# A banded attention's mask: on VectorE with the maximum, or as accumulating matmuls in three of four head groups

## The reference

```python
# x: (4, 2048, 256); 16 heads of 16; WINDOW = 128, one global token
attend = abs(i - j) <= 128 | (i < 1) | (j < 1)
x = x + 0.5 * ffn(layernorm(x))      # top 2 of 8 experts; one with over 1280 tokens is dropped
h = layernorm(x)
q, k, v = (h @ W.T, split in heads, for W in (Wq, Wk, Wv))
logits = where(attend, q @ k.T / 4, -inf)
x = x + (softmax(logits) @ v, heads joined) @ Wo.T
x = x + 0.5 * ffn(layernorm(x))
```

## Time and profile before

| | |
|---|---|
| median of three runs | 870.89 us (870.79 to 871.8) |
| span of the profiled execution, first to last instruction | 867.2 us |
| mean granted TensorE clock | 0.997 |
| TensorE, VectorE, ScalarE, GpSimd busy | 94%, 87%, 73%, 56% |
| first strip's matmuls | at 26.4 us |
| last strip's matmuls | at 794.5 us |

### The profile page before, as it was taken

The page is one execution under the profiler, slowest core; times in us unless marked ns, Lnnn a source line. Parts: engine busy times, 40 slices in busy tenths (PEclk is TensorE's granted clock), DMA queues, the critical chain, the costliest instruction groups (busy, mean ns, idle before and its releaser), DMA issues. The chain is left out here.

```text
span 867.2 us, 50607 instructions
## 1 busy us (share of the span) xinstructions
PE 814.6 (94%) x21504; PEld 606.9 (70%) x21505; DVE 758.3 (87%) x2819; ACT 637.2 (73%) x1417; POOL 488.1 (56%) x874
## 2 busy tenths in 40 slices
PE   9798999999999999999999999898999999999894
PEld 8555667767777777667778777666778777766572
DVE  7898899989887899998987899998988889998785
ACT  2268888897877667998877666898777766888850
POOL 3212556675555557765554465675554556656763
PEclk9999999999999999999999999999999999999998
DMA  7722224432212344441213335352222335220113
GB/s 231 116 81 75 67 73 121 135 88 70 77 62 96 111 146 119 120 127 62 89 51 101 106 105 161 108 131 71 74 73 68 106 93 149 94 77 18 49 51 102
DMA packets 93191, 83.51 MB, mean 96 GB/s; under 512 B 17568, under 2 KB 92192, under 8 KB 92960
## 3 DMA queue, kind: packets, MB, share of 16 engines
q1 hardware_dynamic: 91360, 78.91, 30.1%
q10 hardware_dynamic: 1600, 1.31, 1.0%
HBM read 20.66 MB, written 8.39 MB: 33 GB/s over the span
## 5 line engine op out<-in xcount | busy, mean ns | idle before, releaser
L1105 ACT ACTIVATE probs<-bank 128x384 f32<-128x384 f32 (+1 forms) x1024 | 462.8, 480 | 146.8 <-PE bank L962 137.4
L1431 DVE CUSTOM_DVE_ANT_0 bank<-bank,con 128x288 f32<-128x288 f32 x1024 | 494.4, 518 | 53.2 <-PE bank L934 44.8
L934 PE MATMUL bank<-k_stack,q_stack 96*32 96x288 bf16 x4096 | 325.4, 288 | 10.7 <-DVE row_max L1431 5.7
L962 PE MATMUL bank<-q_stack,k_stack 99*32 99x288 bf16 (+2 forms) x4096 | 319.8, 285 | 16.0 <-ACT probs L1105 9.7
L980 PE MATMUL bank<-probs,v_sb 128*32 128x128 f32 x5888 | 305.4, 272 | 3.6 <-issue 1.5
L1218 POOL TENSOR_SCALAR_AFFINE_SELECT probs<-probs 128x512 f32<-128x512 f32 x240 | 154.8, 645 | 180.1 <-ACT probs L1105 179.5
L980 PEld LDWEIGHTS bank<-probs,v_sb 128*32 128x32 f32 x5888 | 192.1, 110 | 36.7 <-issue 5.3
L962 PEld LDWEIGHTS bank<-q_stack,k_stack 99*32 99x32 bf16 x4096 | 123.6, 95 | 79.7 <-ACT probs L1105 53.5
L934 PEld LDWEIGHTS bank<-k_stack,q_stack 96*32 96x32 bf16 x4096 | 127.3, 95 | 74.0 <-DVE row_max L1431 21.3
L1223 POOL TENSOR_SCALAR_AFFINE_SELECT probs<-probs 128x512 f32<-128x512 f32 x240 | 154.1, 642 | 19.3 <-ACT probs L1105 19.2
L823 PE MATMUL bank<-xnT,wqk_sb 128*32 128x256 f32 x2048 | 158.1, 379 | 0.6 <-DVE neg_max L1453 0.5
(11 more groups left out here) (126 smaller groups left out, 737.2 us busy)
## 6 DMA issues: line engine op xcount, KB each, us to landing
q_stack<-pieces SPq DMA_DIRECT2D x384, 64.0 KB, 2.7
k_stack<-pieces SPq DMA_DIRECT2D x364, 64.0 KB, 2.7
x_ring<-in_x SPq DMA_DIRECT2D x28, 512.0 KB, 4.5
out_x<-x_ring SPq DMA_DIRECT2D x16, 512.0 KB, 3.9
attn<-in_x SPq DMA_DIRECT2D x4, 512.0 KB, 6.0
wback_sb<-in_wback SPq DMA_DIRECT2D x8, 256.0 KB, 6.0
k_stack<-pieces ACTq DMA_DIRECT2D x20, 64.0 KB, 3.6
q_stack<-neg_max SPq DMA_DIRECT2D x48, 16.0 KB, 2.3
```

Of the source, the lines that this page charges most:

```text
L934: last = pe.matmul(a_ring[i % len(a_ring)][SP * s:SP * (s + 1), 0:WIN], q_stack[g % 2][0:KROWS, h, q:q + SP], k_stack[g % 2][0:KROWS, h, q ...
L962: last = pe.matmul(b_ring[i % len(b_ring)][SP * s:SP * (s + 1), start:final], k_stack[g % 2][0:SROWS, h, WINDOW + P * j + SP * s:WINDOW + ...
L1105: act.activation(probs[:, j % 4, h, c0:c1], b_ring[i % len(b_ring)][:, c0:c1], ACT.Exp, scale=LOGIT_SCALE).then_inc(S["exp_ready"], 1)
L1431: dve.tensor_tensor_reduce(out=a_ring[i % len(a_ring)][:, 0:WIN], in0=a_ring[i % len(a_ring)][:, 0:WIN], in1=mask, scale=1.0, scalar=con[: ...
```

## The change

In the first, third and fourth head group of each batch (`g % NG != 1`), `A` no longer closes the bank after the four score matmuls. Further matmuls accumulate the mask on them: the stationary operand is a bf16 identity (a quarter of its columns for each quarter of the partitions), the moving one the bf16 mask. They cover only the columns in which the mask isn't zero. For a middle tile these are the first and the last 32 of 288 columns, in one matmul of 2 x 32. For a group's first tile they are 128 columns and 32, in two matmuls, and for its last tile 32 and 128. VectorE then does a plain maximum (`tensor_reduce`) and writes nothing back. The second group (`g % NG == 1`) keeps the old instruction.

ScalarE makes the two bf16 copies (identity and masks) at the start. The band's DMA has a semaphore of its own for that, at its old place in the queue. TensorE's first `A` waits for the two copies; VectorE's first `A` no longer waits for the set-up loads. The order of events is unchanged.

```diff
+        ident_half = sb("ident_half", [P, P], BF16)
+        band_half = sb("band_half", [P, 3, WIN], BF16)
...
+        def masked_by_products(g):
+            return g % NG != 1
+        def mask_of(t):
+            return 0 if t == 0 else 2 if t == NT - 1 else 1
+        def both_edges(strip):
+            return strip.rearrange("p (b c) -> p b c", c=SP)[:, 0:2 * WINDOW // SP + 1:2 * WINDOW // SP, :]
+        def mask_parts(t):
+            if t == 0:
+                return lower_half, upper_edge
+            if t == NT - 1:
+                return lower_edge, upper_half
+            return both_edges,
...
-                                (con[:, C_BAND:C_PICK], consts[:, C_BAND:C_PICK]),
+                        sp.dma_start(con[:, C_BAND:C_PICK], consts[:, C_BAND:C_PICK]).then_inc(S["band_in"], 16)
...
                             if first and n == 0 and h == 0:
                                 pe.wait_ge(S["pads_ready"], 1)
+                                pe.wait_ge(S["masks_ready"], 2)
...
-                                                 start=True, stop=True)
+                                                 start=True, stop=not masked_by_products(g))
+                            for parts in mask_parts(t) if masked_by_products(g) else ():
+                                for s in range(4):
+                                    strip = a_ring[i % len(a_ring)][SP * s:SP * (s + 1), 0:WIN]
+                                    last = pe.matmul(parts(strip), ident_half[:, SP * s:SP * (s + 1)],
+                                                     parts(band_half[:, mask_of(t), :]),
+                                                     start=False, stop=parts is mask_parts(t)[-1])
                             last.then_inc(S["a_full"], 1)
...
+                        act.wait_ge(S["ident_in"], 16)
+                        act.activation(ident_half[:, :], ident, ACT.Copy).then_inc(S["masks_ready"], 1)
+                        act.wait_ge(S["band_in"], 16)
+                        act.activation(band_half[:, :, :], band_all, ACT.Copy).then_inc(S["masks_ready"], 1)
...
-                            if first and n == 0 and h == 0:
-                                dve.wait_ge(S["setup_in"], 16 * 5)
...
+                            if masked_by_products(g):
+                                dve.tensor_reduce(row_max[:, g % 2, h, t:t + 1], strip, AX.X, ALU.max)\
+                                   .then_inc(S["a_free"], 1)
+                            else:
+                                dve.tensor_tensor_reduce(
+                                    out=strip, in0=strip, in1=band_all[:, mask_of(t), :],
...
```

More of the change, by code:

```diff
@@ L121, in build @@
         take = ident.rearrange("p (h c) -> p h c", c=SP)[:, :, 0:VW]
-        band = [con[:, C_BAND + i * WIN:C_BAND + (i + 1) * WIN] for i in range(3)]
+        band_all = con[:, C_BAND:C_BAND + 3 * WIN].rearrange("p (i c) -> p i c", i=3)
         pick = con[:, C_PICK:C_PICK + NG * SP].rearrange("p (g c) -> p g c", g=NG)
@@ L134, in build @@
         names = ["setup_in", "ident_in", "wqk_in", "pick_in", "ones_ready", "wo_in", "half_ready", "x_first0", "x_first1", "x_first2", "x_first3", "x_ring0", "x_ring1", "x_ring2",
-                 "wqk_ready", "pads_ready", "k_ones", "v_pads", "wback_in",
+                 "wqk_ready", "band_in", "masks_ready", "pads_ready", "k_ones", "v_pads", "wback_in",
                  "stats_ready", "moments_ready", "eps_added", "rstd_ready", "shift_ready", "xn_ready",
@@ L367, in pv_count, with lower_half, lower_edge, upper_half @@
             return g * (3 * NT - 2) + min(3 * i + part, 3 * NT - 2)
+        def masked_by_products(g):
[4 more added lines that the diff above has]
+            return strip.rearrange("p (b c) -> p b c", c=SP)[:, 0:2 * WINDOW // SP + 1:2 * WINDOW // SP, :]
+        def lower_half(strip):
+            return strip[:, 0:WINDOW]
+        def lower_edge(strip):
+            return strip[:, 0:SP]
+        def upper_half(strip):
+            return strip[:, WIN - WINDOW:WIN]
+        def upper_edge(strip):
+            return strip[:, WIN - SP:WIN]
+        def mask_parts(t):
[4 more added lines that the diff above has]
+            return both_edges,
         def window(j):
@@ L832, in _ @@
                                 if first and b == 0 and t == 0:
-                                    pe.wait_ge(S["setup_in"], 16 * 5)
+                                    pe.wait_ge(S["setup_in"], 16 * 4)
                                 pe.wait_ge(*emptied("XT", early_index[b, t // 4], t % 4 // 2))
@@ L1422, in _ @@
                             g, t = divmod(n, NT)
-                            mask = band[0 if t == 0 else 2 if t == NT - 1 else 1]
                             i = HG * n + h
-                            if first and n == 0 and h == 0:
-                                dve.wait_ge(S["setup_in"], 16 * 5)
                             if h == 0 and t == 0 and g >= 2:
@@ L1429, in _ @@
                             dve.wait_ge(S["a_full"], i + 1)
[L1431 to L1434, removed]
+                            strip = a_ring[i % len(a_ring)][:, 0:WIN]
+                            if masked_by_products(g):
[4 more added lines that the diff above has]
+                                    out=strip, in0=strip, in1=band_all[:, mask_of(t), :],
+                                    scale=1.0, scalar=con[:, C_LOWEST:C_LOWEST + 1], op0=ALU.add,
+                                    op1=ALU.max, accum_out=row_max[:, g % 2, h, t:t + 1]).then_inc(S["a_free"], 1)
                         elif kind == "MAX":
```

## The result

| | before | after |
|---|---|---|
| median of four runs each | 871.35 us (870.79 to 873.92) | 913.95 us (909.94 to 915.25) |
| span of the profiled execution | 867.2 us | 913.2 us |
| mean granted TensorE clock | 0.997 | 0.992 |
| ratio after to before | | 1.0475, interval 1.0447 to 1.0504 |

The change costs 43 us. I had predicted 867 us in the median.

A forecast was written before the change was run, and what follows sets the result against it. It took TensorE and VectorE to bound the kernel in turns, by head group. Terms of -5.4, -0.9, +1.2 and 0 summed to -5.1 us, taken as -4: span 863 us, median 867 us, 8-in-10 range 856 to 886.

The forecast's parts named there:

- What the change adds to TensorE: Masked groups: 3,456 product matmuls in 864 sets, about 0.03 us a set up to 64 columns; 28.6 us, 2.4 a group.
- The straight line's 45 us: Higher estimate of the products' TensorE time, set cost drawn straight from 1 column to 288: 0.05 and 0.07 us a set.
- What the exchange is worth: Masked groups: TensorE +2.4 us against VectorE -3.9 each, priced by rates from group windows; sum -5.1 us, taken as -4.
- The rate a: Length a group gains per added microsecond on TensorE: 0.25 from fourth and third groups, 0.75 between first and second.
- What it takes from VectorE: Masked groups: plain maximum stepped at 0.375 us, not 0.43, giving back 46 us, 3.9 a group; bounds 23 and 77.
- b: Length of a group per microsecond on VectorE: 0.39 from fourth and third groups, halved for first groups.
- The opening: Start of the kernel: ScalarE's two bf16 copies fit its idle time, ending near 10 us; uncovered they'd cost 1 us.
- TensorE becomes the bound: Rival, masked groups: TensorE limits there too, a at 0.75 everywhere and b 0.2; +12 us, 883 us, chance 0.32.
- Weight loads aren't hidden: Rival, masked groups: loads between short and long sets exposed, 82 us on TensorE; +52 us, 923 us, chance 0.05.
- The waits for strips vanish whole: Rival: TensorE's 27 us of waits for VectorE's strips go, plus 5 for earlier bank release; -13, 858 us, chance 0.11.
- Nothing measurable: Rival, whole kernel: TensorE's added work and VectorE's relief cancel; 871 us, chance 0.15.
- those for "wrong": Sets at 0.05 us or more, reduction step 0.40 or more, first groups over 1 us longer, or growing waits for exponentials.

The follow-up runs named there:

- e2: Changed kernel without the mask products, keeping the plain maximum over all 288 scores in three of four groups: 861.05 us, ratio 0.986.
- e5: e2 plus 6,912 weight loads that nothing uses, as many instructions as products and their loads: 909.49 us, or 906.12 without one slow execution.
- e9: Changed kernel with eight one-column products a set in place of four, so the mask isn't applied: 994.57 us, ratio 1.1428.
- e6: Changed kernel with two one-column products a set in place of four products, the mask mostly left out: 887.27 us, ratio 1.0183.
- e7: e2 with the plain maximum in the second groups as well, no products: 862.9 us, ratio 0.989.
- e1: Changed kernel with one full-width product matmul in place of each four quarter-width ones, same result: 1016.04 us, ratio 1.1629.
- e8: Changed kernel with two half-width products a set in place of four quarter-width ones, same result: 1028.56 us, ratio 1.1795.

## Why the prediction was wrong

**What the change adds to TensorE: right as array time, wrong as a price.** A set does take 0.03 us: from its start to that of the next line it is 32 ns in the median of 463 sets of four. TensorE's matmuls in the opening, after:

```profile
36.33 0.31 PE L974 MATMUL bank<-k_stack,q_stack 96*32 96x288 bf16 x4
36.46 0.20 PE L981 MATMUL bank<-band_half,ident_half 128*32 128x64 bf16 x4
36.49 0.60 PE L862 MATMUL bank<-xnT,wqk_sb 128*32 128x256 f32 x8
```

The scores ahead take 0.13, against 0.12 before. The floor of 25 ns for a start, for which the prediction cited the Trainium skill, doesn't hold for these quarter-width matmuls. **The failed step is the sentence "I take 28.6, because loads are quick enough in number".** It asked how fast the engine can take loads and matmuls, never how fast they can be brought; that term stood at nothing, without a reason. The prediction charged the products 0.25 to 0.5 of their 28.6 us, 10.8 us in all. They cost 52.9 (e2 to after), and 6,912 loads with no array time in the matmuls' queue cost 45 (e5). The straight line's 45 us and the unhidden loads' 82 were bounds on the same wrong quantity. The whole prediction has no row on the instruction queue.

**What the exchange is worth: the second half of the failure.** The rate a, 0.25 to 0.75, came from windows of the kernel before, all of which had the stream to spare. In the earlier trace rows a first group issues 1,343 + 1,335 instructions in 47.5 us, 4.54 us a block; the fourth 4.77, the third 4.96, the second 4.86. After, they are at 4.16 (first), 4.29 (third) and 4.05 (fourth). With the 4.1 us that lies among them, the result can be worked out again. A masked group gets 288 matmuls and 288 loads, 2.25 blocks or 9.2 us of stream, and its slack is what it had above 4.1 us a block. First: 10.5 blocks need 42.9 of 47.5 us, slack 4.6, so +4.6 (measured +5.6). Fourth: 9.9 blocks, 40.7 of 47.4, slack 6.7, so +2.5 (measured +2.1). Third: 10.2 blocks, 41.7 of 50.4, slack 8.7, so +0.5 (measured +3.0; that work comes in bursts within a group may be why, but isn't shown). The 4.1 is read from the result, so this is an account and no forecast, and it is off by 2.5 us for the third.

The prediction gave first groups +0.4, third -0.3, fourth -0.9. The sign is wrong for the two last, and the first is too small by more than ten times.

**What it takes from VectorE: right as time of an instruction, too high as a price.** The plain maximum lasts 450 ns (460 predicted), and its step, in VectorE's timeline after, is 0.73 / 2 = 0.365 us (0.375 predicted), which is also the median of 346 of them that waited for nothing:

```profile
402.76 0.82 DVE L1479 TENSOR_REDUCE row_max<-bank 128x1 f32<-128x288 f32 x2
403.49 0.42 DVE L1316 BATCH_NORM_STATS2 stats<-x_ring 128x6 f32<-128x256 f32 x1
```

The busy time fell by 45 us, 50 to 90 predicted. By the step it is 768 x 0.065 = 50 us; e2 turned it into some 12 us of the time, a rate of 0.24. The prediction had b = 0.39 for third and fourth groups and half of that for first ones. That makes 16 us, from which it took back 1.1 for the fall of b with VectorE's load; b was too high by some 4 us.

**The opening: covered, as predicted.** ScalarE's copies end at 10.05 us ("near 10"). The first strip starts at 26.8 us, 0.4 later than before; e2 has the same copies and starts at 26.0.

**The rivals.** *TensorE becomes the bound* (883, chance 0.32) had the right sign and engine but not the mechanism: first groups have 2.7 us of idle TensorE where this case needed none, and e5 costs 45 us with no product matmul at all. *Weight loads aren't hidden* (923) is nearest in time; e5 shows that loads cost nearly as much with no products beside them (45 of 53 us), but by their number as instructions: they take 97 ns each, as before, and what stops is both queues together. *The waits for strips vanish whole* came true in the main (27 to 8.8 us), but gave no time. *Nothing measurable* is ruled out by the 43 us.

**The signs.** Of those for "right", the set's 0.03 us, the step, the waits for strips, VectorE's waits for TensorE and the second groups' 55 us held. VectorE's busy time fell by 45 us, just under the 50 of the sign, and the fourth groups, which were to shorten by about 1 us, grew by 2. Of those for "wrong", first groups grew by more than 1 us; the waits for exponentials fell. So of the signs against, one spoke, and it doesn't say why: all of them looked at the engines of the exchange. A set of 0.03 us with a far longer kernel is what none of them had foreseen. Where the sum was off by 47 us, the rise from 7 to 33 us in the issue rows was the only view that held it.

**What stays open.** Why a block takes some 4 us is answered in part by the traces. In the changed kernel's trace, the matmul behind each of the 43 gaps starts 2.1 to 3.1 us (median 2.5) after the start of the latest packet. The next packet starts 1.05 us or more after that matmul (median 1.3). Together that is 3.2 us at the least, near the closest start of two packets, and 3.8 in the middle, near the best average of sixteen in a row. e9's 71 gaps give the same (2.3 to 3.3, median 2.6; then 1.05 or more, median 1.3). Over all 184 blocks between 30 and 840 us the next packet starts behind the block's first instruction in 178, up to 0.3 us ahead of it in six. It suggests that a block is asked for only about when TensorE begins the one before, so that the engine has one block in advance and no more. No run varied this, and why the 2.1 us are needed isn't shown: a packet itself takes 0.9 to 1.8 us, and no run here varied the load on the DMA engines.

## What to carry to other kernels

Count an engine's instructions, not only its busy time: divide a stretch's matmuls and loads by 256 and look at the microseconds a block. In this kernel, near 4.1 us each further TensorE instruction cost about 16 ns, a matmul with its load 32, however short; at 4.5 to 5.0, as before, there was slack for some. To see in a trace whether the stream is dry, look for gaps without a semaphore that are 256 instructions apart, or a multiple, in matmuls and loads together. An instruction that rides beside others at 7.5 ns of array time isn't cheap if it is one of thousands.

A split of a change is worth a run each: here VectorE's half (861 us, or 863 in all four groups) beats both the kernel before and the changed one, since the probabilities are masked later anyway and, on these inputs, the mask in the maximum wasn't needed.

## What the runs showed of the hardware

- **TensorE can run out of instructions** in a straight-line program. 16 KB blocks of 256 instructions start no closer than 3.3 us before and after (3.2 in e2, e6 and e7; in e1, near the end of its span, one pair is 1.7 apart), and sixteen in a row took at least 3.78 us each (e9) and 3.89 (after), while the engine can issue one in 2.6. The Trainium skill ("Runtime: NRT & Kernel Launch", Instruction fetch mechanics) says that instructions come in 16 KiB blocks of 256, which the packets here agree with, and that crossing a boundary is mostly hidden; after, it cost 0.5 to 2.8 us at 43 of them.
- **A change of tile width between neighbouring matmuls** costs about 0.2 us a set of products (e1, e8). Counted as array time at 0.03 us a set, e1's 864 products would be an estimated 26 us; e1 costs 155 above e2.
- **A maximum over 288 values in a bank** is stepped at 0.365 us, against 0.43 for the fused add and maximum with its accumulator read the earlier trace rows.
